# Another order on VectorE in the experts of a decoder layer: the gate product ahead of the low halves of an older tile

## The reference

```python
logits = jnp.einsum('ed,btd->bte', gate_w, x)
scores = jax.nn.sigmoid(logits) + gate_b
weights, indices = jax.lax.top_k(scores, TOP_K)      # 4 of 16 experts
weights = weights / weights.sum(-1, keepdims=True)
...
h1 = jnp.einsum('btd,edc->btec', x, w1_routed)       # 256 -> 176
h2 = jnp.einsum('btd,edc->btec', x, w3_routed)
h3 = jax.nn.silu(h1 * h2)
experts_out = jnp.einsum('btec,ecd->bted', h3, w2_routed)
routed_out = jnp.einsum('bted,bte->btd', experts_out, router_probs)
return shared_out + routed_out
```

## Time and profile before

| | |
|---|---|
| median of 3 runs | 844.42 us (840.83 to 850.3) |
| span of the profiled execution | 847.7 us |
| expert phase, from the first load (SP) to the end | 513.7 to 847.7 us |
| TensorE busy over the span | 78% (664.4 us) |
| VectorE busy | 67% (569.3 us) |
| ScalarE busy | 47% (402.3 us) |
| GpSimd busy | 54% (459.9 us) |
| mean granted TensorE clock | 0.904 of full speed |

### The profile page before, as it was taken

The page is one execution under the profiler, slowest core; times in us unless marked ns, Lnnn a source line. Parts: engine busy times, 40 slices in busy tenths (PEclk is TensorE's granted clock), DMA queues, the critical chain, the costliest instruction groups (busy, mean ns, idle before and its releaser), DMA issues. The chain is left out here.

```text
span 847.7 us, 15795 instructions
## 1 busy us (share of the span) xinstructions
PE 664.4 (78%) x4034; PEld 555.8 (66%) x4034; DVE 569.3 (67%) x1747; ACT 402.3 (47%) x1136; POOL 459.9 (54%) x363
## 2 busy tenths in 40 slices
PE   1888679883578988785736355799999999999994
PEld 1777667763455656453524224699999999999993
DVE  5799769933667666452614665777777777777774
ACT  3866346211256545242322134555555555555552
POOL 3566665460005455535334550667777776777775
PEclk9999889997579999787958677999999999999997
DMA  9900001213125546622212353477777787787774
GB/s 295 290 23 26 26 13 38 87 51 118 44 100 192 190 139 236 240 72 100 73 65 88 130 180 103 75 124 130 133 132 133 127 134 125 130 140 126 140 113 57
DMA packets 77094, 100.38 MB, mean 118 GB/s; under 512 B 9744, under 2 KB 70304, under 8 KB 76448
## 3 DMA queue, kind: packets, MB, share of 16 engines
q0 software_dynamic: 26736, 37.64, 25.2%
q1 hardware_dynamic: 48096, 59.64, 22.7%
q10 hardware_dynamic: 2176, 2.10, 0.8%
HBM read 50.97 MB, written 52.95 MB: 123 GB/s over the span
## 5 line engine op out<-in xcount | busy, mean ns | idle before, releaser
L1562 POOL DMA_INDIRECT out_dram<-yw,xg x143 | 225.1, 1574 | 116.1 <-issue 61.0
L1184 POOL DMA_INDIRECT xs_scratch<-rows,slot x128 | 125.0, 977 | 172.6 <-issue 91.8
L1445 PE MATMUL cbank<-w_hi,xtc_hi 128*128 x286 | 107.4, 375 | 7.9 <-DVE xtc_lo L1457 7.8
L1445 PE MATMUL cbank<-w,stc_hi 112*128 (+1 forms) x572 | 111.9, 289 | 1.0 <-DVE stc_hi L1527 0.8
L1505 ACT ACTIVATE sgc<-hh 128x128 f32<-128x128 f32 x143 | 44.4, 311 | 129.8 <-DVE hh L1499 96.9
L1457 DVE TENSOR_TENSOR xtc_lo<-cbank,xtc_hi 128x256 fp32r<-128x256 f32 x143 | 60.6, 424 | 60.4 <-ACT xtc_hi L1452 49.1
L355 POOL TENSOR_TENSOR pv<-v_sb,pr 128x256 f32<-128x256 f32 (+7 forms) x32 | 68.5, 2154 | 58.1 <-DVE pr L344 39.8
L1445 PEld LDWEIGHTS cbank<-w,stc_hi 112*128 112x128 f32 (+1 forms) x572 | 92.9, 189 | 5.4 <-issue 3.6
L1445 PE MATMUL cbank<-w,xtc_hi 128*128 x286 | 93.2, 326 | 0.0
L1445 PE MATMUL cbank<-w_hi,xtc_lo 128*128 x286 | 92.5, 324 | 0.0
L1445 PEld LDWEIGHTS cbank<-w_hi,xtc_hi 128*128 128x128 f32 x286 | 54.0, 189 | 23.0 <-issue 11.0
(11 more groups left out here) (223 smaller groups left out, 1577.6 us busy)
## 6 DMA issues: line engine op xcount, KB each, us to landing
xg<-xs_scratch SPq DMA_DIRECT2D x143, 144.0 KB
w<-w13r_dram SPq DMA_DIRECT2D x8, 704.0 KB
w_hi<-ctx_t_dram SPq DMA_DIRECT2D x8, 512.0 KB
x_scratch<-x_all SPq DMA_DIRECT2D x16, 256.0 KB, 2.1
w_hi<-x_scratch SPq DMA_DIRECT2D x8, 512.0 KB, 5.7
out_dram<-w SPq DMA_DIRECT2D x16, 256.0 KB
w<-w2r_dram SPq DMA_DIRECT2D x4, 1024.0 KB
x_all<-x_dram SPq DMA_DIRECT2D x12, 256.0 KB
```

What stands on the lines that cost most here:

```text
L1184: nc.gpsimd.indirect_dma_start(t["xs"], bass.IndirectOffsetOnAxis(ap=slot[:, n % 2, k:k + 1].bitcast(U32), axis=0), rows[:, n % NROW, k // ...
L1445: last = nc.tensor.matmul(out, stationary, moving, start=j == 0, stop=j == len(pairs) - 1)
L1562: nc.gpsimd.indirect_dma_start(t["out"], bass.IndirectOffsetOnAxis(ap=xg[:, p, ID:ID + 1].bitcast(U32), axis=0), yw[:, p % YB, :], None, c ...
```

## The change

One number in `plan`: `s_lo_` gets the place 1.3 in place of 0.7, and so comes behind `hh_` (1.2) in VectorE's order of a step. Before, VectorE issued in step i `t_lo` of tile i-3, `s_lo_` of i-6, `hh_` of i-4, `y_ev` of i-7; after, it issues `t_lo` of i-3, `hh_` of i-4, `s_lo_` of i-6, `y_ev` of i-7. The other engines' orders, all waits, buffers and instructions stay.

```diff
@@ -1566,7 +1566,7 @@
         plan = [(0, "y", 0, load), (0, "g", 8, scatter),
                 (-1, "s", 0, split_hi), (-1, "v", 0, split_lo),
                 (0, "t", 3, t_mm), (0.1, "s", 3, t_hi), (0.2, "v", 3, t_lo),
-                (0.5, "t", 6, s_t), (0.6, "s", 6, s_hi_), (0.7, "v", 6, s_lo_),
+                (0.5, "t", 6, s_t), (0.6, "s", 6, s_hi_), (1.3, "v", 6, s_lo_),
                 (1, "t", 4, h_mm), (1.1, "s", 4, h2_), (1.2, "v", 4, hh_), (1.3, "s", 4, sg_),
                 (4, "t", 7, y_mm), (4.1, "v", 7, y_ev)]
```

## The result

The changed kernel takes 823.02 us (median of 4 runs, 819.73 to 825.84) against 847.36 us of the kernel before, with one more run of it than was shown above. The ratio is 0.971, with an interval of 0.967 to 0.976. The profiled execution has a span of 824.0 us against 847.7, 23.7 us less.

A forecast was written before the change was run, and what follows sets the result against it. The prediction took a ring of ScalarE and VectorE to bound the expert steps, TensorE just behind. 15.0 (long stretch) + 6.3 (split steps) - 0.7 (end) = 20.6 us off 844.42 gave 823.8 us, range 816 to 832.

The forecast's parts named there:

- the ring: ScalarE and VectorE starts in an expert step, claimed to close in 2.14 us, set the pace and fall to 1.66.
- The long stretch: 130 expert steps without splits: step falls from 2.149 to 2.035 us, TensorE setting the pace, saving 15.0 us.
- The upper bound: Most the 130 steps without splits could save: 20.8 us, if each gained the shown step's 0.16 us.
- The bound from the weight loads: Steps without splits: by the busy time of TensorE's weight loads, gain at most 15.6 us, about 822 us at best.
- the lower bound of 12.4: Least gain in us over 130 steps without splits, from weight-load holes before h_mm, 0.095 us a step.
- The split steps: Ten expert steps with splits: from 3.00 to 2.37 us each, saving 6.3 us.
- The new wait: Low halves queue behind hh_, which waits for h_mm and h2_; slack 0.48 us before y_mm, cost nothing.
- The end: After the last output: GpSimd's last scatter lags more, taking 0.7 us off the gain (between 0 and 3).
- A: Rival: GpSimd becomes the bound in the long stretch, 2.10 us a tile, 8.5 us lost, about 832 us; chance 12%.
- B: Rival: TensorE's 0.14 us before h_mm is its own, only steps with splits gain, 838 us; chance 8%.
- C: Rival: another wait in the ring holds hh_ in both parts, so no effect, 844 us; chance 4%.
- D: Rival: low halves come too late for y_mm and hold TensorE; slower, about 851 us; chance 3%.

The follow-up runs named there:

- long_stretch_only: Against the kernel before, the new order only from tile 10 on, the old order in the steps with splits; ratio 0.975.
- low_halves_last: Against the changed kernel, both low-half instructions moved further back, behind y_ev (place 4.2 instead of 1.3); ratio 1.010 to the kernel before.
- one_half_moved: Against the kernel before, only the second low-half instruction (L1527) moved behind hh_, the first left ahead; ratio 0.973.
- splits_hidden: Against the changed kernel, splits of w2 moved: ScalarE's part between h2_ and silu, VectorE's to the end of its step; ratio 0.972 to the kernel before.

## Why the prediction was right

The predicted median was 823.8 us, the measured one is 823.02. The nearness is partly luck. The sum said 20.6 us, the two profiles differ by 23.7 and the medians by 24.3; the sum was 3 us short, and the median of before, from which it was taken off, rose by 2.9 (from 844.42 to 847.36) with the fourth run. By steps:

- *The bound was the ring, not TensorE.* Right, and shown from both sides by the extra transpose: nothing in the kernel before, 0.11 us a tile in the changed one. The row that decided it was the 0.15 us between the end of `t_lo` and the start of `h_mm`, with the 0.27 us of the earlier trace rows for comparison.
- *The long stretch.* Right in kind, too small: 15.0 us expected, 130 x 0.144 = 18.8 measured. The term that was mis-sized is TensorE's own step, 2.035 in place of 2.005. The wait ahead of `h_mm` itself, 0.115 us a step in the sum, was nearly right: the mean distance from the last transpose to the second `h_mm` over the 130 steps fell from 0.39 to 0.27 us, by 0.12. The other 0.025 us lies behind it, in `h_mm` and around the start of `y_mm`: from the first matmul of `y_mm` to the one that reads `stc_lo` 0.257 us became 0.243, and the longest distances from the last `h_mm` to `y_mm`, 0.19 to 0.33 us in nine steps of 130, became 0.17 at most. I had left these short gaps in TensorE's issue as they were, and they went too; why is open. The upper bound, 20.8, was nearer than the value taken.
- *The bound from the weight loads.* The prediction read "at most 15.6 us" off them, and the stretch gained 18.8. The holes were not all of the delay: the same 1949 loads were busy for 263.73 us before and 260.56 after, so 3.2 us of waiting stood inside their own rows. 15.6 and 3.2 together are the gain. The same goes for the lower bound of 12.4 us from the holes ahead of `h_mm`.
- *The split steps.* The 2.37 us is as read off. Ten of them were to bring 6.3 us. From the first load to the end of the long stretch the phase is 318.33 us before and 294.12 after, 24.2 us less; less 18.8, the steps with splits brought 5.4. Eight steps of 0.63 us, those between the first `y_ev` and the ninth, are 5.0 of it; of the ten counted, the ones at the edges brought less, and one of them took 2.49 us.
- *The new wait.* The slack of the low halves was put at 0.48 us. In the rows after they end at 703.95, are seen 0.14 later, and are due at 704.56: 0.47. The cost was nothing, as said.
- *The end.* 0.7 us was taken off for a longer lag of the last scatter. The lag grew by 0.38 us, but what follows the long stretch is 15.75 us in place of 15.7, so the term was worth 0.05.
- *Outside the change.* The experts began 0.46 us later in the profiled execution of after (first load 514.13 in place of 513.67): 18.8 + 5.4 - 0.05 - 0.46 = 23.7, the difference of the spans.

Of the rivals, A (GpSimd) did not come, and one memset showed room of at least 0.05 us a tile; two showed that it was near. B and C fell with the extra transposes and the steps. D did not come at this place, but its price was real one place further on: behind `y_ev` the same two instructions made the kernel slower by 1.0% than before, where D had named 0.8% (851 us), though through a ring and not through lateness alone, so that the nearness of the two numbers is chance.

## What to carry to other kernels

When an engine looks full and others look idle, take the starts of one step, go around the engines from each wait to its releaser, and see whether the chain comes back to where it began in exactly one step; what closes is the likely bound, and a little work added to the engine that looks full tests it. An instruction on the ring is worth about its distance from start to start, until the next bound is reached. Then do the same for the new order, with every wait that the moved instruction now stands behind: slack in a single pass is not enough, since a pass that feeds the next one closes into a ring of its own. And an order on an in-order engine is to be chosen by who waits outside: first what another engine stands still for, then what is needed a step later.

## What the runs showed of the hardware that was not expected

- Scatters took 2.00 us on GpSimd in the split steps before, and 1.55 us in the same steps after. In the kernel before they began while VectorE's split ran; in the changed one they begin after it. Row pairs of the kernel before and then of the changed one:

```profile
541.81 0.69 DVE L1415 TENSOR_TENSOR w<-w 128x512 fp32r<-128x512 f32 x1 [0.70 <-ACT w L1409]
541.93 2.00 POOL L1562 DMA_INDIRECT out_dram<-yw,xg  x1 [1.00 <-DVE yw L1548]
```

```profile
538.73 0.69 DVE L1415 TENSOR_TENSOR w<-w 128x512 fp32r<-128x512 f32 x1
539.48 1.55 POOL L1562 DMA_INDIRECT out_dram<-yw,xg  x1 [0.82 <-DVE yw L1548]
```

  In `long_stretch_only`, which has the old order there, eight scatters are busy 15.34 us, in the changed kernel 12.01. The split reads two operands from SBUF. The Trainium skill's page "SBUF — State Buffer", section "Who interferes with whom", says that a VectorE instruction with two SBUF inputs contends with a GpSimd instruction that reads SBUF, and that the order of issue decides which one is blocked. By that rule, the trace agrees: the scatter reads its row numbers from SBUF, begins second and is longer by 0.45 us. The same section says that a probe saw no DMA stalled by a `tensor_tensor`, which the split is; here the 2.00 us beside such an instruction stand against that.

  The other profiles narrow it down. The scatters that begin 0.11 to 0.14 us behind the start of a split take 2.00 to 2.02 us in all five kernels that have such ones, `low_halves_last` among them, whose only change, against the changed kernel, is the place of `s_lo_`. Those that begin 0.56 us behind it, with 0.13 us of the split left, take 1.55 in `one_half_moved`. In `splits_hidden`, which differs from the changed kernel by the place of the splits alone, the split begins 1.0 to 1.3 us into the scatter, and the scatter takes 1.55 as well. So the cost goes with a scatter that starts early in a split. That a port is the reason no run here shows.
- The start distance of two VectorE instructions depends on the pair. L1527, the second low half, works on partitions 64 to 127, and it and the one behind it start when the one before has ended: 0.29 to 0.30 us behind an instruction of 0.28, and 0.32 to 0.33 behind one of 0.29. The other pairs of a step overlap by 0.08 us: `t_lo` to the first low half 0.34 at a length of 0.42, `hh_` to `y_ev` 0.26 at 0.34, and in `one_half_moved` the first low half to `hh_` 0.20 at 0.28. That is why taking L1527 out gave back more than its own length. Whether the partitions are the reason was not tested.
- A full matmul row hid 15.6 us of holes in the weight loads, 263.73 busy of 279.37 us, and the holes in turn hid 3.2 us of waiting. The distance of starts, 0.27 us in a step that was not held against 0.41 in most others, showed the size of the wait ahead of `h_mm` directly.
